# Attention and mixture of experts on one core: the q chain and the shifted scores one unit later, two DVE steps first in their unit

## The reference, cut to what matters

```
xn = layernorm(x)                                   # over t
q, k, v = split(transpose(xn) @ w_in.T + b_in)      # t x (8 heads x 16)
scores = q k^T / 4, only where |i - j| <= 64
attn = softmax(scores)
o = attn v, then @ w_out.T + b_out
y = relu(transpose(o)) * ctx
x = x + w_ct^T y + b_ct
x = x + moe(layernorm(x))
```

## Time and profile before

| | |
|---|---|
| median of 3 runs | 779.32 us (775.33 to 782.4) |
| the profiled execution | 774.11 us, its span 772.4 us |
| busy, share of the span | PE 87%, DVE 52%, ACT 46%, POOL 56% |
| chain that ended last | PE 73%, DVE 11%, DMA 5%, issue 5% |
| mean granted TensorE clock | 0.962 |
| attention stage | to about 400 us; full periods of eight units from about 95 to 305 us |

### The profile page before, as it was taken

How to read it: one execution, slowest core, us unless ns; L and a number is a source line. 1 busy time by engine, 2 the same in 40 slices (tenths; PEclk the granted TensorE clock), 3 DMA queues, 4 the chain that set the end, 5 groups by cost and what they waited for, 6 DMA issues and landing times.

```text
span 772.4 us, 14074 instructions
## 1 busy us (share of the span) xinstructions
PE 672.9 (87%) x4136; PEld 330.5 (43%) x4136; DVE 401.6 (52%) x1439; ACT 354.9 (46%) x670; POOL 436.2 (56%) x640
## 2 busy tenths in 40 slices
PE   3378889999999999888769969989999999999992
PEld 1235545555555555543334535433333333333330
DVE  3388888888888888862333286222322222222210
ACT  3227666666666666555212212224454444444441
POOL 2567788787877777756210000114775766758653
PEclk9999999999999999998979989999999999999996
DMA  9823334433333334211577652533555555554420
GB/s 329 208 69 100 100 100 114 113 106 99 104 100 105 108 111 114 80 31 32 210 324 256 238 174 66 170 105 69 120 110 127 133 132 118 111 137 80 83 43 0
DMA packets 64472, 95.17 MB, mean 123 GB/s; under 512 B 18064, under 2 KB 42768, under 8 KB 62224
## 3 DMA queue, kind: packets, MB, share of 16 engines
q1 hardware_dynamic: 50048, 66.75, 28.3%
q0 software_dynamic: 9600, 18.89, 12.9%
q10 hardware_dynamic: 4752, 8.65, 3.3%
HBM read 50.99 MB, written 19.14 MB: 91 GB/s over the span
## 4 chain that ended last, share of the span: by engine, by line
PE 73%; DVE 11%; DMA 5%; issue 5%; POOL 2%; SPq 2%; ACT 1%; ACTq 0%; DVEq 0%; POOLq 0%
PE bank L731 18%; PE bank L761 9%; PE bank L718 6%; PE bank L585 5%; PE bank L555 5%; PE bank L571 4%; DVE bank L1100 4%; PE bank L635 4%; PE bank L749 3%; PE bank L711 3%; DMA xn_rows<-xn 3%; PE bank L612 2%; PE bank L742 2%; PE bank L606 2%; PE bank L597 2%
## 5 line engine op out<-in xcount | busy, mean ns | idle before, releaser
L1100 DVE CUSTOM_DVE_ANT_0 bank<-bank,cb 128x192 f32<-128x192 f32 (+1 forms) x512 | 187.1, 415 | 50.4 <-PE bank L555 48.9
L899 ACT ACTIVATE wgu<-bank 128x384 f32<-128x384 f32 (+1 forms) x256 | 125.3, 545 | 57.1 <-PE bank L571 56.7
L731 PE MATMUL bank<-wgu,rowsT 128*64 x320 | 147.4, 604 | 2.7 <-DVE X L1343 2.3
L733 PE MATMUL bank<-X,rowsT 128*64 128x512 f32 x320 | 147.5, 604 | 0.0
L1329 DVE TENSOR_TENSOR act_in<-act_in,bank 128x256 f32<-128x256 f32 x56 | 23.6, 421 | 212.6 <-ACT act_in L985 212.5
L492 POOL DMA_INDIRECT rows<-xn_rows,gather_i x40 | 43.9, 1096 | 128.3 <-issue 116.2
L555 PE MATMUL bank<-wgu 96*128 96x192 bf16 (+1 forms) x512 | 95.8, 273 | 20.9 <-DMA wgu<-wgu 11.3
L441 POOL TENSOR_SCALAR_AFFINE_SELECT wgu<-wgu 128x512 f32<-128x512 f32 (+1 forms) x128 | 74.7, 584 | 64.3 <-ACT wgu L899 64.0
L508 POOL DMA_INDIRECT out<-y_out,scatter x40 | 63.4, 1584 | 36.1 <-DMA out<-y_out,scatter_i 17.4
L571 PE MATMUL bank<-wgu 99*128 99x192 bf16 (+1 forms) x512 | 73.0, 264 | 11.9 <-DMA wgu<-wgu 6.9
L508 POOL DMA_INDIRECT out<-y_out,scatter_i x40 | 61.0, 1525 | 39.0 <-issue 20.6
(11 more groups left out here) (170 smaller groups left out, 1013.1 us busy)
## 6 DMA issues: line engine op xcount, KB each, us to landing
wgu<-wgu SPq DMA_DIRECT2D x192, 128.0 KB, 2.5
wgu<-w_gu SPq DMA_DIRECT2D x16, 1024.0 KB, 7.8
X<-w_d SPq DMA_DIRECT2D x16, 512.0 KB, 4.0
out<-y_out ACTq DMA_DIRECT2D x17, 256.0 KB, 4.5
wgu<-ctx SPq DMA_DIRECT2D x16, 256.0 KB, 3.0
xn_rows<-xn SPq DMA_DIRECT2D x16, 256.0 KB, 2.4
rows<-xn_rows ACTq DMA_DIRECT2D x16, 256.0 KB, 2.8
X<-x SPq DMA_DIRECT2D x1, 3072.0 KB, 15.8
```

The source lines that it names most:

```text
L731: mm(gb[k.buf][0:GROUP, :], rowsT[:, k.buf, c, 0:GROUP], wgu[:, bass.ds(e * 2048 + 512 * c, 512)], start=(c == 0), stop=(c == 3))
L733: last = mm(gb[k.buf][GROUP:P, :], rowsT[:, k.buf, c, GROUP:P], gu_half[:, k.buf, 512 * c:512 * c + 512], start=(c == 0), stop=(c == 3))
L899: nc.scalar.activation(probs[j % 4][:, 2 * half:2 * half + 2, 0:w], s2[half][:].rearrange("p (j c) -> p j c", j=2)[:, :, 0:w], ACT.Exp, sc ...
L1100: last = v.tensor_tensor_reduce(o, o, cb[:, B_MASK + off:B_MASK + off + w], 1.0, MASKED * 2.0, ALU.add, ALU.max, rowmaxes[n % 2][:, h + i, ...
```

## The change

Each step of the q chain moves by one unit: `project_q` from -13 to -12, `first_q` and `residue_q` to -11, `second_q` and `third_part` to -10, the copies to -10, -9, -8 and -7. The shifted scores, the exponentials and the zeroing move from 11 to 12; the attend step stays at 14, so it has one unit less behind them. On DVE, `add_attention` and `max_rows` stand ahead of everything else in their unit. No instruction is added or removed.

```diff
 SP   step(U)
-                if (n := at(U, -11)) is not None:
+                if (n := at(U, -10)) is not None:
                     after(sp, s2_ready, 2 * UNITS * (n - RING + 1))
                     sp.wait_ge(q_p1, n + 1)
                     send_q(n, (0,))
-                if (n := at(U, -10)) is not None:
+                if (n := at(U, -9)) is not None:
                     send_q(n, (1, 3))
-                if (n := at(U, -9)) is not None:
+                if (n := at(U, -8)) is not None:
                     sp.wait_ge(q_p2, n + 1)
                     send_q(n, (2, 4))
-                if (n := at(U, -8)) is not None:
+                if (n := at(U, -7)) is not None:
                     sp.wait_ge(q_p3, n + 1)
                     send_q(n, (5,))
 POOL step(U)
-                if p := piece(U, 11):
+                if p := piece(U, 12):
                     cut_band(*p)
-                if (n := at(U, -11)) is not None:
+                if (n := at(U, -10)) is not None:
                     third_part(n, qres, qparts, q_p2, q_p3)
 PE   step(U)
-                if p := piece(U, 11):
+                if p := piece(U, 12):
                     shifted_scores(*p, 0)
                     shifted_scores(*p, 1)
-                if (n := at(U, -13)) is not None:
+                if (n := at(U, -12)) is not None:
                     project_q(n)
 ACT  step(U)
-                if (n := at(U, -12)) is not None:
+                if (n := at(U, -11)) is not None:
                     first_q(n)
-                if (n := at(U, -11)) is not None:
+                if (n := at(U, -10)) is not None:
                     second_q(n)
-                if p := piece(U, 11):
+                if p := piece(U, 12):
                     exponentials(*p)
 DVE  step(U)
+                if (n := at(U, 33)) is not None:
+                    add_attention(n)
+                if (n := at(U, 9)) is not None:
+                    max_rows(n)
                 if p := piece(U, -1):
                     maximum(*p, 0)
                 if (n := at(U, 40)) is not None:
                     logits_out(n)
                 if (n := at(U, -8)) is not None:
                     residue_k(n)
-                if (n := at(U, 33)) is not None:
-                    add_attention(n)
-                if (n := at(U, 9)) is not None:
-                    max_rows(n)
...
-                if (n := at(U, -12)) is not None:
+                if (n := at(U, -11)) is not None:
                     residue_q(n)
```

## The result

The changed kernel takes 797.88 us in the median of four runs (795.99 to 800.38), the kernel before 780.82 us beside it (775.33 to 782.4). The ratio is 1.0273, 95% interval 1.0233 to 1.0314: slower, as forecast, but by 17 us (medians) to 21 us (ratio) where 9 were forecast. A ratio leaves out every execution that took over 1.5% longer than the fastest of the same kernel, a median here does not, so the two can differ.

The account below looks back on a forecast made before the run. TensorE was taken as nearly the bound (busy 18.41 of 20.3 us a period), DVE and POOL also full. -11.9 + 8.7 + 8.7 = +5.5, plus 4 for the clock, +9.5: 788 us on the median, own range 786 to 794, overall 768 to 801.

Parts of the forecast that it names:

- (a): From mix_channels to project_v: DVE adds to x first, project_v's wait goes; -0.99 us a period, -11.9 us in all.
- (b): Units 3 and 4: project_q loses its cover, TensorE waits for DVE before second scores; +0.83 us a period, +8.7 us.
- (c): Unit 0: the attend step waits for POOL's later zeroing, delaying mix_channels; +0.87 us a period, ten times, +8.7 us.
- Start and drain of the stage have no term: Both ends of the attention stage: queue order stays and latency rules, so no cost counted; +-1.5 us.
- (d): TensorE's clock around unit 4's sparse stretch: two or three falls at 1.6 us each, +4 us; ends 0 and 17.6.
- R3: Rival: TensorE's clock falls in each period, +5.5 + 17.6 = +23, 802 us; chance 0.10.

Follow-up runs that it names:

- e6: The kernel before with only the shifted scores, exponentials and zeroing one unit later: 789.8 us, ratio 1.0134.
- e3: The changed kernel without the q chain's move (DVE's order and the later scores, exponentials and zeroing stay): 781.8 us, ratio 0.9996 to the kernel before.
- e2: The changed kernel with five zero-weight products in TensorE's unit 4 wait for DVE, sequences 2 to 14: 781.5 us, ratio 1.0014 to the kernel before.
- e12: The kernel before with three zero-weight products in unit 3's wait for the copied maxima, sequences 1 to 15: 772.45 us, ratio 0.9897.
- e10: The changed kernel run once more, unaltered, beside the unit 7 filler variant: 808.66 us, ratio 1.0269 to the kernel before.
- e4: The kernel before with DVE's order alone (add to x and copied maxima first): 777.9 us, ratio 0.9952.
- e9: The changed kernel with five zero-weight products in unit 7, where TensorE has no wait, sequences 2 to 14: 791.71 us, ratio 1.0184 to the kernel before.
- e7: The kernel before with only the q chain one unit later: 798.1 us, ratio 1.019.
- e8: e4 with five zero-weight products in unit 3's wait for the copied maxima, sequences 2 to 14: 760.09 us, ratio 0.9774 to the kernel before.

## Why the prediction went wrong in size

Of the 23.9 us between the two profiled executions the forecast had 9.5. The 14.4 that it missed are 1.2 in the waits of the ten periods (6.7 against 5.5), 3.8 in their falls (7.8 against 4), 4.4 in the start, 4.7 in the drain and 0.3 in the experts.

*(a) DVE's order, -0.99 a period.* Mechanism right: L612 no longer waits for L1124, project_v starts 1.97 after mix_channels. Price with the shift in place -0.86 (21.07 in e6 to 20.21 in e3), alone -0.75: less than forecast in both.

*(b) The q chain, +0.83.* Right: waits of 0.41 and 1.20 us in unit 4, project_q behind them; +0.76 measured from e3 to the changed kernel. No DMA wait is left.

*(c) The later zeroing, +0.87.* Right: mix_channels 9.26 after unit 5 (9.3 forecast), L585 waits 0.52 for L443; +0.77 alone. Two small errors cancel in the 9.3: POOL's block started at 1.83 and not 1.71, and lasted 6.80 and not 6.98. The forecast's own numbers give +0.91 (9.3 less 8.39) and not the +0.87 that it added.

Their sum, 21.0 a period, was 20.97. This part of the walk stands, though the sum is closer than its three terms: beside -0.86, +0.76 and +0.77 they were 0.13, 0.07 and 0.10 too large in size. On the median the forecast was 779.32 + 9.5, which is 788.8 and not 788.

*Failed: "Start and drain of the stage have no term".* The start has one. The first mix_channels came at 107.1 instead of 102.7, and at 105.9 in e2. The attend steps of the first sequences wait for POOL too, 3.5 us in all before 108 us, among it 0.96 us at 68.41 and 1.02 at 106.57. I had counted POOL's wait only where gate and the third part of q are in its block; it needs only the missing unit of slack. About 3 us is my estimate; single executions don't give it better, as e12, whose start has neither part of the change but some of the filling products, came to the same point at 105.1 and the kernel before at 102.7. The drain's 4.7 us are falls of the clock: in e2, with two of them, it took 82.1 us, less than the 83.9 of the kernel before.

*Failed: "I take two or three falls, +4 us" in (d).* The price was right (0.55 of the clock behind the 1.20 us wait, 1.6 to 1.7 us each) and so was the place, for four of the five falls in the full periods. The number was not: five there, and more in the drain. Filling that one wait takes 2.5% off (1.0273 to 1.0014). The comparison with e12 gives an estimate of the budget without the clock: 1.0014 / 0.9897 = 1.012, 9 us, which is 10 x 0.67 plus the start's 3. The rest, 1.0273 / 1.012 = 1.015, 12 us, is the clock's part, net of what the kernel before lost to it. It is an estimate because both filled kernels still have falls (e2 at 361 and 388 us, e12 at 353 and 387) and were filled in different waits. Forecast were 5.5 and 4; by this estimate it was 9 and 12. I had judged how often the clock falls by one stretch that did and one that did not, though the change repeats the sparse one 11 times. The time of R3, to which I gave 0.10, was nearer than the forecast's; its mechanism, a fall in each period, held in e10's profiled execution and not in the first one.

The Trainium skill ("TensorE: Matmul & The Clock Gate", section "HAM oscillation — how this bites in real kernels") describes a loop that is throttled in each pass. Five falls in ten periods lie between that rule and my two or three; by the rule the time was 802, measured 797.9. In e10's profiled execution, with a fall in each period, the trace agrees with the rule, and the time was 817.84 us: a fall there lasted longer and cost 2.9 us a period (23.9 less 20.97), not 1.6.

*The expectations.* e2's effect was twice as large as expected, since three of the drain's five falls went as well; e4 beat its expected period of 20.0, because I had let the DMA decide alone and had left out that project_q's own wait goes; e9's time was overestimated.

What stays open: how the start's 3 us divide between q chain and shift (e6 104.2, e7 106.8, e3 103.2, e4 103.7 to the first mix_channels, each with other falls; the waits for POOL in it are 2.6 us in e6 and e3 and 1.0 in e7), what sets the number of falls in an execution, and which falls the kernel before has in the executions that were not profiled; its times go from 773 to 787 us.

## What to carry to other kernels

Walk one period through all in-order queues before moving a step: the step that leaves a stretch in which its engine had to wait anyway (project_q in unit 3) loses its cover, and one unit taken from a three-engine relay is a new wait even if each engine has idle time. Where a change makes a stretch of TensorE sparse in every period, price the clock for every period, and count both kernels' falls, in more than one execution, before believing a difference. A wait that can't be taken away may be filled with products of zero weights into a bank that is accumulating anyway; here that was worth 1.0% (e12), 1.8% (e4 to e8) and 2.5% (the changed kernel to e2), and with DVE's order 2.3% over the kernel before.

## What the runs showed of the hardware

Falls of the clock can recur with the loop, but not at a fixed rate: in e4's profiled execution they came in every second period (151, 192, 233 and 274 us), in the changed kernel's at 117, 161, 247 and 312 us, in e10's in each period. A wait of 1.2 us between small products was enough in these executions, and it was not followed by a fall each time (225.34 us in the changed kernel). Products whose weights are all zero kept the granted clock up (e2, 1.00 over 210 us, beside 0.97 without), and the same products in a dense stretch did not (e9, 0.97).
